# Paired-head attention in a decoder kernel: one 64-row half of the array, one score product and one PSUM bank for each head of a pair

## The reference

```python
# L1_attn: 16 heads, q and k of 8 features, v of 64 features
P = softmax(q_h @ k_h.T)            # 512 x 512 for each head
o_h = P @ v_h
# L1_ffn's attention: 16 heads, q, k and v of 8 features, with a causal mask
P = softmax(where(causal, q_h @ k_h.T, -inf))
```

## Time and profile before

| | us |
|---|---|
| three executions | 2521.09, 2524.52, 2524.91 (median 2524.52) |
| span of the profiled execution, first to last instruction | 2517.6 |
| its PE busy, share of the span | 2087.0 (83%) |
| its DVE busy | 1221.4 (49%) |
| its ACT busy | 981.2 (39%) |
| its POOL busy | 542.7 (22%) |
| mean granted clock of TensorE | 0.93 of full speed |

### The profile page before, as it was taken

The page is one execution under the profiler, slowest core; times in us unless marked ns, Lnnn a source line. Parts: engine busy times, 40 slices in busy tenths (PEclk is TensorE's granted clock), DMA queues, the critical chain, the costliest instruction groups (busy, mean ns, idle before and its releaser), DMA issues.

```text
span 2517.6 us, 32350 instructions
## 1 busy us (share of the span) xinstructions
PE 2087.0 (83%) x10674; PEld 1247.4 (50%) x10674; DVE 1221.4 (49%) x2784; ACT 981.2 (39%) x2084; POOL 542.7 (22%) x433
## 2 busy tenths in 40 slices
PE   4697897877987988878888987887988968979888
PEld 3345544534454455544544555444545644445556
DVE  5443343345755453456554534574644256636443
ACT  2222222225433443544244535432544354326343
POOL 2572373200440020014300200242011003420110
PEclk8899999988998998989989998898999989989999
DMA  6000000000000000000000000000000000000000
GB/s 168 1 0 1 0 0 0 0 0 1 1 1 1 1 1 1 6 0 1 1 1 1 1 1 6 1 1 1 1 1 1 1 6 1 1 1 1 1 1 5
DMA packets 17978, 13.59 MB, mean 5 GB/s; under 512 B 7323, under 2 KB 14463, under 8 KB 17823
## 3 DMA queue, kind: packets, MB, share of 16 engines
q1 hardware_dynamic: 17631, 11.58, 1.7%
q10 hardware_dynamic: 192, 0.02, 0.0%
HBM read 10.55 MB, written 1.05 MB: 5 GB/s over the span
## 4 chain that ended last, share of the span: by engine, by line
issue 63%; PE 17%; POOL 7%; DVE 5%; POOLq 5%; DVEq 1%; DMA 0%; ACT 0%; SPq 0%
PE PSUM L1158 3%; PE PSUM L410 2%; POOLq L841 2%; PE PSUM L458 2%; PE PSUM L443 2%; DVE maxparts L578 2%; POOL KRING L629 2%; POOLq L843 2%; POOL OTA L840 2%; POOL OTA L845 2%; PE PSUM L426 1%; PE PSUM L467 1%; PE PSUM L1168 1%; POOL rstd L217 1%; PE PSUM L1145 1%
## 5 line engine op out<-in xcount | busy, mean ns | idle before, releaser
L571 DVE TENSOR_REDUCE negmax<-PSUM 128x1 f32<-128x512 f32 (+3 forms) x512 | 293.7, 589 | 192.9 <-PE PSUM L413 106.6
L558 ACT ACTIVATE PTA<-PSUM 128x1024 f32<-128x1024 f32 (+3 forms) x256 | 220.4, 864 | 241.2 <-PE PSUM L443 155.3
L217 POOL TENSOR_TENSOR rstd<-var,neg_half 128x4 f32<-128x4 f32 (+1 forms) x38 | 38.4, 1011 | 1162.4 <-DVE var L209 1162.4
L410 PE MATMUL PSUM<-KRING,QSTACK 96*128 96x512 f32 (+3 forms) x512 | 199.5, 417 | 1.5 <-ACT QSTACK L526 0.3
L629 POOL TENSOR_TENSOR KRING<-OTA,ones_col 32x512 fp32r<-32x512 f32 x128 | 132.1, 1032 | 259.1 <-PE PSUM L446 128.9
L443 PE MATMUL PSUM<-QSTACK,KRING 128*128 128x512 f32 (+3 forms) x512 | 175.1, 413 | 4.4 <-ACT QSTACK L531 2.3
L1158 PE MATMUL PSUM<-PTA,VA 128*64 128x512 f32 x512 | 141.3, 631 | 0.0
L410 PEld LDWEIGHTS PSUM<-KRING,QSTACK 96*128 96x128 f32 x512 | 98.0, 192 | 85.0 <-DVE negmax L571 46.5
L1502 ACT ACTIVATE PTA<-PSUM,V 128x512 f32<-128x512 f32 x128 | 88.0, 687 | 133.3 <-PE PSUM L1272 133.0
L1200 PE MATMUL PSUM<-KMA,QXA 128*128 128x512 f32 x256 | 133.9, 605 | 5.4 <-ACT VA L1477 2.7
L1720 DVE TENSOR_REDUCE nmax<-PSUM 128x1 f32<-128x589 f32 x128 | 98.7, 771 | 71.9 <-PE PSUM L1201 64.0
(11 more groups left out here) (374 smaller groups left out, 4296.8 us busy)
## 6 DMA issues: line engine op xcount, KB each, us to landing
W<-in_L_ffn_W_dram SPq DMA_DIRECT2D x1, 2048.0 KB
out_dram<-X SPq DMA_DIRECT2D x4, 256.0 KB, 2.3
PTA<-in_L_attn_Wc_dram SPq DMA_DIRECT2D x1, 640.0 KB
PTA<-in_L_attn_Wo_dram SPq DMA_DIRECT2D x1, 512.0 KB
Wkv<-in_L_xattn_Wkv_dram SPq DMA_DIRECT2D x1, 512.0 KB
KMA<-in_L_attn_ttt_proj_dram SPq DMA_DIRECT2D x1, 256.0 KB
QXA<-in_L_ffn_w_up_dram SPq DMA_DIRECT2D x1, 256.0 KB
QXA<-in_L_ffn_w_down_dram SPq DMA_DIRECT2D x1, 256.0 KB
```

The source lines that it names most:

```text
L410: last = T.matmul(bank(j % 2, w), QSTACK[0:96, s, t * P:(t + 1) * P], KRING[0:96, (2 * s + e) % 6, 0:w], start=True, stop=not a.causal)
L558: A.activation(a.probsT(s, c), PSUM[:, 2 + 2 * (k % 2):4 + 2 * (k % 2), 0:SEQ - a.first(c)], ACT.Exp) .then_inc(m_exp, 1)
L571: Vv.tensor_reduce(negmax[:, s % 2, e, t:t + 1], bank(j % 2, a.width(t)), AX.X, ALU.max, negate=True) .then_inc(m_max, 1)
```

## The change

- Queries and keys now both lie on 128 rows: head 0 of a pair in rows 0 to 63 and head 1 in rows 64 to 127 (its parts in rows 96 to 127, rows 32 to 95 are for the maxima). A product takes the 64 rows of its head alone, so nothing has to be zero for it, and `KRING` and POOL's `keys` go. `paired_pool` is no longer called for `causal`.
- `scores(n)` makes one query tile for both heads, into two neighbouring banks, and one DVE reduction takes both (128x2 out of 128x2x512). There are 32 steps instead of 64 in a stage. The first six and the odd tiles use banks 0 and 1, the others banks 2 and 3.
- `scores_T` has banks 4 and 5 alone, so it waits for the exponential just before it.
- `turn_maxima` has 128x128 operands in fp32r instead of 128x4 in fp32; `max_rows` is two copies of 32 rows instead of one of 4.
- In `causal` both heads' products come first and both masks after them.
- The orders are new, and the semaphore waits with them. Setup constants on POOL change.

The diff, cut to its core:

```diff
-        KRING = sb("KRING", [P, 6, SEQ], F32R)
-        maxparts = sb("maxparts", [P, 2, QT, 2, 2], F32R)
+        maxparts = sb("maxparts", [P, 2, QT, P], F32R)
...
-        full = Paired(0, False, "v v p p v p v t p t v t t v p t t v p t t v p t t p t x t")
-        causal = Paired(1, True, "p p p t t p t t p t t p t t p x t t p t t")
+        full = Paired(0, False, "p p v v" + 6 * " t p v" + " x t")
+        causal = Paired(1, True, "p p" + 6 * " t p" + " x t")
+
+        def score_banks(n):
+            return 0 if n < 6 or n % 2 else 2
...
+                if n:
+                    pe.wait_ge(m_max, 4 * a.stacks(b, 0) + (n if n < 6 else n - 1))
+                for e in range(2):
+                    rows = slice(64 * e, 64 * e + 64)
+                    last = T.matmul(bank(k + e, w), QSTACK[rows, s, t * P:(t + 1) * P], KSTACK[rows, s, 0:w],
+                                    start=True, stop=not a.causal)
                 if a.causal:
-                    last = T.matmul(PSUM[:, j % 2, t * P:(t + 1) * P], ident_bf[:, :], causal_bf[:, :], start=False, stop=True)
+                    for e in range(2):
+                        last = T.matmul(PSUM[:, k + e, t * P:(t + 1) * P], ident_bf[:, :], causal_bf[:, :],
+                                        start=False, stop=True)
...
                 for t in range(QT):
-                    last = T.matmul(PSUM[96:100, 7, t * P:(t + 1) * P],
-                                    maxparts[:, s % 2, t, :, :].rearrange("p e w -> p (e w)").bitcast(F32), ident[:, :],
+                    last = T.matmul(PSUM[:, 7, t * P:(t + 1) * P], maxparts[:, s % 2, t, :], ident_r[:, :],
                                     start=True, stop=True)
...
-                if k >= 2:
-                    pe.wait_ge(m_exp, 4 * a.stacks(b, 0) + k - 1)
+                if k >= 1:
+                    pe.wait_ge(m_exp, 4 * a.stacks(b, 0) + k)
                 w = SEQ - a.first(c)
                 for e in range(2):
-                    dst = PSUM[:, 2 + 2 * (k % 2) + e, :]
-                    last = T.matmul(dst[:, 0:w], KRING[:, (2 * s + e) % 6, c * P:(c + 1) * P], QSTACK[:, s, a.first(c):SEQ],
+                    rows = slice(64 * e, 64 * e + 64)
+                    last = T.matmul(bank(4 + e, w), KSTACK[rows, s, c * P:(c + 1) * P], QSTACK[rows, s, a.first(c):SEQ],
                                     start=True, stop=not a.causal)
...
-                A.activation(QSTACK[96:100, s, :], PSUM[96:100, 7, :], ACT.Copy).then_inc(m_rows, 1)
+                for first in (32, 64):
+                    last = A.activation(QSTACK[first:first + 32, s, :], PSUM[first:first + 32, 7, :], ACT.Copy)
+                last.then_inc(m_rows, 1)
...
-                    if c == 2 and s + 1 < PAIRS:
+                    if c == 1 and s + 1 < PAIRS:
                         max_rows(s + 1)
...
-                Vv.tensor_reduce(negmax[:, s % 2, e, t:t + 1], bank(j % 2, a.width(t)), AX.X, ALU.max, negate=True)                    .then_inc(m_max, 1)
+                Vv.tensor_reduce(negmax[:, s % 2, t, :], PSUM[:, k:k + 2, 0:a.width(t)], AX.X, ALU.max, negate=True)\
+                    .then_inc(m_max, 1)
...
-            def keys(s):
-                for e in range(2):
-                    rows = slice(LANE * e, LANE * (e + 1))
-                    g.tensor_tensor(KRING[rows, (2 * s + e) % 6, :], KSTACK[rows, s, :],
-                                    ones_col[rows, 0:1].to_broadcast([LANE, SEQ]), ALU.mult).then_inc(m_keys, 1)
```

More of the change, by code:

```diff
@@ L87, in decoder_kernel @@
         PTA = sb("PTA", [P, 7680])
+        with nc.sbuf_tensor("KSTACK", [P, PAIRS, SEQ], F32R) as KSTACK:
+            pass
         OTA = sb("OTA", [P, 4096])
@@ L469, in spread, with tile @@
                 last.then_inc(m_spread, 1)
-            def tiles(first, n):
-                for i in range(first, min(first + n, 8 * PAIRS)):
-                    scores(i // 8, i % 8)
-            n = {"v": iter(range(8)), "p": iter(range(PAIRS)), "t": iter(range(12)), "x": iter(range(1))}
+            def tile(n):
+                if n < 4 * PAIRS:
+                    scores(n)
+            n = {"v": iter(range(8)), "p": iter(range(PAIRS)), "t": iter(range(7)), "x": iter(range(1))}
             for step in a.opening:
-                {"v": project_values, "p": pick, "t": lambda i: tiles(i, 1), "x": turn_maxima}[step](next(n[step]))
+                {"v": project_values, "p": pick, "t": tile, "x": turn_maxima}[step](next(n[step]))
@@ L479, in paired_tensor @@
             for s in range(PAIRS):
-                ahead = 8 * s + 12
+                ahead = 4 * s + 7
+                odd = s % 2 == 1
                 scores_T(s, 0)
-                tiles(ahead, 1)
-                if s:
+                tile(ahead)
+                if s and not a.causal:
                     value(s - 1, 3)
-                tiles(ahead + 1, 1)
-                if s >= 2 and not a.causal:
-                    spread(s - 2)
+                elif s and not odd:
+                    value(s - 1, 2)
@@ L488, in paired_tensor @@
                 scores_T(s, 1)
-                tiles(ahead + 2, 2)
-                value(s, 0)
-                scores_T(s, 2)
-                tiles(ahead + 4, 1)
-                if a.causal and s + 1 < PAIRS:
-                    turn_maxima(s + 1)
-                value(s, 1)
-                if not a.causal and s + 1 < PAIRS:
-                    turn_maxima(s + 1)
-                tiles(ahead + 5, 1)
-                scores_T(s, 3)
-                tiles(ahead + 6, 1)
-                value(s, 2)
@@ L502, in paired_tensor @@
-                tiles(ahead + 7, 1)
-                if s and not a.causal:
-                    sums(s - 1)
-            value(PAIRS - 1, 3)
+                tile(ahead + 1)
+                if not a.causal:
+                    value(s, 0)
+                elif s and not odd:
+                    value(s - 1, 3)
+                if s + 1 < PAIRS:
+                    turn_maxima(s + 1)
+                scores_T(s, 2)
+                tile(ahead + 2)
+                if not a.causal:
+                    value(s, 1)
+                    if s >= 2:
+                        spread(s - 2)
+                elif odd:
+                    value(s, 0)
@@ L506, in paired_tensor @@
+                scores_T(s, 3)
+                tile(ahead + 3)
+                if not a.causal:
+                    value(s, 2)
+                    if s:
+                        sums(s - 1)
+                elif odd:
+                    value(s, 1)
             if a.causal:
+                value(PAIRS - 1, 2)
+                value(PAIRS - 1, 3)
                 finish(0, 3)
@@ L587, in normalise, with tile @@
                 Vv.tensor_tensor(OT[:, s, :], OT[:, s, :], bank(7), ALU.mult).then_inc(m_norm, 1)
-            def tiles(first, n):
-                for i in range(first, min(first + n, 8 * PAIRS)):
-                    maxima(i // 8, i % 8)
-                    if i % 8 == 7:
-                        split_maxima(i // 8)
+            def tile(n):
+                if n < 4 * PAIRS:
+                    maxima(n)
+                    if n % 4 == 3:
+                        split_maxima(n // 4)
             def add23(s):
@@ L901, in _ @@
                 norm()
-                paired_pool(pool, b, causal)
                 norm()
@@ L1163, in finish @@
                 def finish(first, n):
+                    if first == 0:
+                        pe.wait_ge(m_max, 4 * full.stacks(b, PAIRS))
                     for s in range(first, first + n):
@@ L1250, in finish @@
                 def finish(first, n):
+                    if first == 0:
+                        pe.wait_ge(m_max, 4 * causal.stacks(b, PAIRS))
                     for g in range(first, first + n):
```

161 lines of the change are left out of this document (76 added, 85 removed).

## The result

The change takes **2571.68 us** (median of 4 runs, 2569.69 to 2574.54) against 2524.72 for the kernel before on the same chips: ratio 1.019, 95% interval 1.0171 to 1.021. It is 1.9% slower, clear of the noise; 2438 was forecast. The profiled execution has a span of 2572.5 us, 54.9 more than before, at a mean granted clock of 0.852 against 0.930.

A forecast was written before the change was run, and what follows sets the result against it. PE was taken as the bound, at full clock. Per batch row `full` would save 20.5 us and `causal` 1, four times that -86: span 2517.6 to 2432, median 2438 us, range 2410 to 2505.

The forecast's parts named there:

- (1): Score products in `full`: the two heads' row halves run at the same time, 1.9 us less for a pair.
- Rival A: Row halves don't run together, each second product costs its 0.24 as now; about 2497 us, chance 0.15.
- (2): `turn_maxima` in `full`: fewer passes but wider weights, 0.6 us instead of 1.0, 0.4 less a pair.
- (3): Maxima in `full`: DVE's split no longer meets POOL's adds, so PE's 1.65 us idle at `turn_maxima` goes.
- (4): Single bank pair for transposed scores: in `full` the new wait, some 1.6 us, is just covered by PE's 1.68 a group.
- (5): DVE's reduction over two banks takes 1.22 us; DVE's some 7.4 us a pair is covered by PE.
- (6): POOL's key copies and the setup cost nothing before or now; POOL's 48 us wait covers a longer setup.
- (7): Opening of `full` gets 3.1 us longer, with PE waiting for split queries and `turn_maxima` for the last values.
- The sum for `full`: Pairs of `full` save 23.6 us in all, the opening loses 3.1: net 20.5 less for a batch row.
- Rival B: Switching between row halves, whole array and column halves costs extra, mainly in `causal`; about 2560 us, chance 0.11.
- The criterion of the masks: Sign in `causal`: the prediction is wrong if masks start 0.3 us or more after the product ahead of them.
- Rival C: `full`'s gain returns as a new wait, its chain of exponentials reaching 2.6 us a group; about 2523 us, chance 0.04.

The follow-up runs named there:

- e16: e15 with each causal product taking its head's 64 rows instead of all 128, same results; 2537.49 us, ratio 1.0061 to the kernel before.
- e15: The change with causal products on 128 rows (masked keys, later masks on GpSimd), two transposed bank pairs, other opening of `full`; 2451.93 us, ratio 0.9714.
- e1: The change with causal's score and transposed products on all 128 rows, mixing the two heads; 2490.2 us.
- e8: The change with `full`'s products on all 128 rows, mixing the two heads, causal left as changed; 2597.5 us.
- e14: e13 with the change's single pair of banks for causal's transposed scores; 2488.6 us.
- e13: e15 with the later key masks made by VectorE, behind the opening and pairs 1 and 3, instead of GpSimd; 2482.1 us.
- e4: The change with causal score tiles in banks 0 and 1 and transposed scores alternating between two bank pairs; 2557.7 us.
- e7: The change with causal score tiles in banks 0 and 1, plus an unused 64-row product behind every transposed causal product; 2616.0 us.
- e11: The change with another opening of `full` alone, two value projections moved forward; 2561.8 us.

## Why the prediction was wrong

The step that failed is the premise ahead of all steps: "The granted clock is 1.00 there, the 2.4 GHz level, so there is nothing to win from the clock." The 1.00 was read rightly, but there was something to lose. Every price in the sum was a price at 2.4 GHz, and the sum asked only how long each instruction takes, not what the clock would do when products use half the rows. e16 against e15 puts it at 17.8 us a batch row, of which the switches, at 8 x 0.09 by the one pair at full clock, are an estimated 0.7, and about 17 the clock. In the change itself e1 against the change shows 21.9 for both. The other 6.6 of the 28.5 are still there in e1: 1.8 in the opening, and 4.9 in the pairs (60.6 against 55.7), where its stretch at half clock and the single banks lie.

By steps:

- (1) *Row halves run together*: right in kind, and 0.19 measured where 0.24 was taken (e8). Rival A is out.
- (2) *`turn_maxima`*: 683.45 to 684.04, 0.59; 0.6 was taken.
- (3) *The hold-up goes*: right, 0.17 for each instruction.
- (4) *One pair of banks*: covered in `full` (10.13 a pair). In `causal` the banks are worth 1.9 us a batch row with the clock at 0.89 (e14 less e13; the intervals of their ratios overlap, their times on one chip don't), and 5.2 at half clock (e4). No pair of runs shows their price with the clock at full all through.
- (5) *Reduction*: 1.22, as taken.
- (6) *Key copies and setup at nothing*: right for the copies. As for the 5.2 us ahead of the first `full`, the copy of `YT` ahead of the one at 619.24 starts at 600.87 before and 605.86 in the change, but at 600.16 in e15, which has the same setup. Over the change and its 16 variants it lies anywhere from 600.16 to 606.99, so they can't be put down to the setup or to anything else in the change. What shifts it was not tried.
- (7) *The opening of `full`*: from the copy of `YT` to the first exponential 29.1 before (619.24 to 648.34) and 34.6 now (624.41 to 659.00): 5.5 longer, 3.1 forecast. The first `turn_maxima` waits as foretold:

```profile
655.80 0.66 PE L434 MATMUL PSUM<-ident_r,maxparts 128*128 128x128 f32 x4 [1.41 <-DVE VA L1786]
```

- *The sum for `full`*: 20.5 forecast, 16.7 measured (15.1 in the first batch row). Of the 5.4 us between forecast and first row, the opening is 2.4 and the first pair 2.7, which at half clock takes 11.57 where it took 8.83; one other pair with a half-clock stretch (11.37 against 10.13) is 1.2, and the other pairs give 1.0 back. So here too the clock has the largest part.
- *`causal`*: 1 gain forecast, 28.5 lost. With whole rows, two bank pairs and the opening mended (e15) it is 87.9, the forecast's 87; that is a coincidence, because it is another kernel.

Rival B named the place rightly and foretold 2560, near the 2572 measured, but not the mechanism: its break-even was 0.1 more for each switch. e16 shows 0.12 for each of the eight switches back to half rows, and no cost in the other direction that the saving doesn't cover; of this, 0.09 a pair is left in the time. That would be 3 us in all, an estimate from one pair, and not enough to turn 2438 into a loss. So its number is near by luck. The criterion of the masks (0.3 or more after the product) struck at once: in the change L448 starts at 896.83, at full clock, and its mask at 897.27, 0.44 later. It pointed to the right stage for the wrong reason. The Trainium skill (TensorEngine Tiling (Array Packing), Key Properties) says a change of tiling mode drains the engine; the trace agrees with a price of 0.12, not with a stall of a whole product.

Rival C is out: pairs of `full` at full clock come 10.13 apart, so the chain of exponentials has not grown to 2.6 a group.

The Trainium skill (TensorE: Matmul & The Clock Gate, Part 1) says that the clock follows how busy TensorE has been. The trace doesn't agree if busy means time: 94% busy at half clock in the change and 99% for 90 us in e7, and 86% (46.62 of 54.34) at full clock in e15. The measurement decides: here the rows in use count as well.

What stays open: how the chip weighs rows in use against idle time. Two halves side by side also fill the rows for half as long as two whole products one after the other, and the runs don't tell a count of rows from a count of rows by time. In `full`, whose value products use all rows and follow every product pair, the same half-row products kept the clock but for short stretches. Its first pair got most of its clock back by whole rows (e8, 9.12) and by another opening with half rows (e11, 9.54). So rows are not the only thing that counts, and the runs don't say where the border lies.

## What to carry to other kernels

A product that uses half the rows can be quick by itself and slow down everything around it: before packing row halves, look at what share of the nearby products use all rows, and after it read the granted clock of that stretch first. Here the same products on all rows, with zeros under the other head, one after the other, took 86 us less than side by side on half of them, 71 of it in the stage itself. Narrow products between whole-array ones gained nothing from running together here (0.32 against 0.30 at 256 columns).

## What the runs showed of the hardware

- The granted clock fell to half with TensorE 94% busy, when the causal products used 64 rows; an unused product on 128 rows brought it back in part (0.66), one on 64 rows didn't (0.50, with TensorE 99% busy).
- fp32r products on rows 0 to 63 and 64 to 127 start within 0.01 us of each other. In `full` a pair of them at 512 columns is 0.19 us shorter than two on 128 rows; from the start of a whole-array mask to the next product it takes 0.21 when that one is on row halves and 0.09 when it is on all rows (e16 and e15).
- GpSimd's product of 128x512 took 1.02 us and its clearing of 64x1024 0.95 in the causal opening, beside VectorE's reductions from PSUM, which kept their 1.22; one of VectorE's small copies took 0.58 in place of 0.17 and ended with a clearing (884.32 and 884.28, e15).
